# M from fp16 halves of Wo and of a kv divided by the K sums, M seven steps behind kv, and f2 of tile 62 in two halves

## The reference

```python
q = elu(q) + 1.0;  k = elu(k) + 1.0          # of layernorm(x) @ Wq, @ Wk
k_sum = k.sum(axis=2)                         # over the 2048 positions
z = einsum('bhnd,bhd->bhn', q, k_sum)[..., None] + EPS
kv = einsum('bhnd,bhne->bhde', k, v)
out = einsum('bhnd,bhde->bhne', q, kv) / z
x = x + out_heads_joined @ Wo + bo
h = square(relu(layernorm(x) @ W_fc.T));  y = h @ W_proj.T
for _ in range(5):                            # mem starts at 0
    mem_new = 0.9 * mem + y - reset;  spk = mem_new > 1
x = x + mean of the five spk
```

## Time and profile before

| | before |
|---|---|
| median of 3 runs | 1036.79 us (1036.23 to 1037.36) |
| the profiled execution | 1036.43 us, its span 1034.6 us |
| TensorE busy | 1026.2 us (99%) |
| VectorE busy | 873.8 us (84%) |
| ScalarE busy | 737.3 us (71%) |
| GpSimd busy | 654.7 us (63%) |

### The profile page before, as it was taken

How to read it: one execution, slowest core, us unless ns; L and a number is a source line. 1 busy time by engine, 2 the same in 40 slices (tenths; PEclk the granted TensorE clock), 3 DMA queues, 4 the chain that set the end, 5 groups by cost and what they waited for, 6 DMA issues and landing times.

```text
span 1034.6 us, 19797 instructions
## 1 busy us (share of the span) xinstructions
PE 1026.2 (99%) x6999; PEld 653.0 (63%) x6999; DVE 873.8 (84%) x1871; ACT 737.3 (71%) x1216; POOL 654.7 (63%) x410
## 2 busy tenths in 40 slices
PE   8999999999999999999999999999999999999998
PEld 4444444444444467777777767777777777777887
DVE  7899887898888699888888888888888888888875
ACT  8888677778768758676666767676767676676664
POOL 1444434455345488777778676878777777777835
PEclk9999999999999999999999999999999999999999
DMA  4546553225323545454454454455444444544441
GB/s 132 148 127 145 121 122 88 77 63 122 87 69 82 122 76 113 93 107 99 96 128 108 82 105 95 105 106 98 97 108 108 93 103 107 108 93 93 78 80 45
DMA packets 265284, 104.24 MB, mean 101 GB/s; under 512 B 219360, under 2 KB 262624, under 8 KB 265184
## 3 DMA queue, kind: packets, MB, share of 16 engines
q1 hardware_dynamic: 265040, 102.90, 44.7%
q10 hardware_dynamic: 144, 0.07, 0.0%
HBM read 33.69 MB, written 16.79 MB: 49 GB/s over the span
## 4 chain that ended last, share of the span: by engine, by line
PE 97%; DMA 1%; DVE 1%; ACT 1%; issue 0%; ACTq 0%; DVEq 0%
PE proj L619 31%; PE acc L784 16%; PE acc L820 16%; PE acc L662 15%; PE acc L759 8%; PE acc L768 4%; PE acc L761 4%; PE proj L696 1%; PE proj L684 1%; DMA xT<-xnat 1%; ACT feat L879 0%; PE acc L633 0%; PE proj L673 0%; DMA x_t<-in_L_attn_x_dram 0%; ACT feat L875 0%
## 5 line engine op out<-in xcount | busy, mean ns | idle before, releaser
L875 ACT ACTIVATE feat<-proj 128x1024 f32<-128x1024 f32 x123 | 125.7, 1022 | 193.7 <-PE proj L619 193.7
L1555 POOL TENSOR_TENSOR qT<-qT,feat 128x1024 f32<-128x1024 f32 x60 | 142.4, 2373 | 174.8 <-DVE xnat L1186 151.3
L1590 POOL TENSOR_TENSOR h<-h_f,h 128x512 f16<-128x512 f32 x128 | 148.8, 1183 | 159.2 <-ACT h L1052 159.2
L784 PE MATMUL acc<-xn2T,wfcT 128*128 128x256 f16 x1536 | 178.0, 273 | 0.0
L820 PE MATMUL acc<-wpT,h 128*128 128x256 f16 (+1 forms) x1560 | 177.9, 271 | 0.1
L662 PE MATMUL acc<-feat,xnat 128*128 128x512 f16 x768 | 176.2, 379 | 0.0
L619 PE MATMUL proj<-wk,xT 128*128 128x512 f16 x756 | 173.3, 379 | 0.7 <-DMA xT<-xnat 0.4
L784 PEld LDWEIGHTS acc<-xn2T,wfcT 128*128 128x128 f16 x1536 | 150.3, 98 | 28.9
L1561 POOL TENSOR_TENSOR feat<-feat,rz 128x1024 f32<-128x1024 f32 x60 | 165.8, 2764 | 2.8 <-DVE rz L1293 2.8
L619 PE MATMUL proj<-wq,xT 128*128 128x512 f16 x720 | 165.2, 379 | 0.0
L820 PEld LDWEIGHTS acc<-wpT,h 128*128 128x128 f16 x1560 | 150.6, 98 | 22.7 <-issue 0.3
(11 more groups left out here) (106 smaller groups left out, 1317.9 us busy)
## 6 DMA issues: line engine op xcount, KB each, us to landing
x_t<-in_L_attn_x_dram SPq DMA_DIRECT2D x128, 128.0 KB, 2.3
xT_spill<-xT SPq DMA_DIRECT2D x64, 128.0 KB, 2.0
out_dram<-out_t SPq DMA_DIRECT2D x63, 128.0 KB, 2.1
xT<-xT_spill SPq DMA_DIRECT2D x60, 128.0 KB, 2.3
ks_all<-ks_rows SPq DMA_DIRECT2D x4, 512.0 KB, 4.5
qT<-feat SPq DMA_TRANSPOSE x120, 3.1
m_all<-in_L_attn_Wk_dram SPq DMA_DIRECT2D x4, 256.0 KB, 4.3
xT<-xnat SPq DMA_TRANSPOSE x64, 2.4
```

Of the source, the lines that this page charges most:

```text
L784: mm = pe.matmul(acc[:, 2 + g % 2, f % 2 * 2 * P:(f % 2 + 1) * 2 * P], wfcT[:, left, f * C2 + c2, :], xn2T[:, pair % 4, right * C2 + c2, : ...
L1555: pool.tensor_tensor(kacc[:, b % 2, :], kacc[:, b % 2, :], k_feat(n), ALU.add).then_inc(k_added, 1)
L1590: pool.tensor_tensor(lo, h_f[:, k % 4, :], hi, ALU.subtract).then_inc(h_lo, 1)
```

## The change

Five things change.

1. `wo` is held as fp16 high and low part, split like the other weights in four pieces at steps 20 to 23 (one ScalarE and one VectorE instruction of 128x512 each), and its DMAs land in `stage`.
2. `kvT`, now with one buffer, is divided by the K sums before M. `load_ks` brings the K sums to all partitions one step behind their store. In step kv + 5 VectorE inverts 512 of them for each half of the partitions (`invert_ks`) and scales kv (`scale_kv`); in step kv + 6 ScalarE makes its high part and GpSimd the low part (`kv_hi_part`, `kv_lo_part`). In the second half the two inversions are at t = 16 and 17, the scaling at 18, the parts at 19. The transpose of the K sums, `rk` and `rks` go.
3. `m_job` makes 24 fp16 matmuls in place of 8 fp32 ones and waits for the low part of kv.
4. In `GUESTS` the M jobs stand seven and nine steps behind kv (before: two and four), the last batch's in `LATE` stay, and the q projections are at 24, 32, 40, 48 (before: 27, 33, 44, 49).
5. f2 of tile 62 is made like that of tile 63, in two halves of 128 columns in two banks (`f2_halves`, `f2_part`), its comparisons in the order of the last tile (`parted_spikes`).

```diff
-        GUESTS = {20: ("kv", 0, 0), 22: ("m", 0, 0), 24: ("m", 0, 1), 27: ("q", 0), 33: ("q", 1),
-                  36: ("kv", 1, 0), 38: ("m", 1, 0), 40: ("m", 1, 1), 44: ("q", 2), 49: ("q", 3),
-                  52: ("kv", 2, 0), 54: ("m", 2, 0), 56: ("m", 2, 1)}
+        GUESTS = {20: ("kv", 0, 0), 24: ("q", 0), 27: ("m", 0, 0), 29: ("m", 0, 1), 32: ("q", 1),
+                  36: ("kv", 1, 0), 40: ("q", 2), 43: ("m", 1, 0), 45: ("m", 1, 1), 48: ("q", 3),
+                  52: ("kv", 2, 0), 59: ("m", 2, 0), 61: ("m", 2, 1)}
...
             def m_job(b, i):
 
-                pe.wait_ge(chain_free, through("kv", b, 0))
+                pe.wait_ge(kv_lo, b + 1)
                 for qq in range(2):
-                    for s in range(2):
-                        for side in range(2):
-                            slot = 4 * s + 2 * i + qq
-                            own = slice(side * DH, (side + 1) * DH)
-                            mm = pe.matmul(m_half(b, i, side, qq)[s * DH:(s + 1) * DH, :],
-                                           kvT[own, b % 2, slot * DH:(slot + 1) * DH], wo[own, slot, :],
-                                           start=True, stop=True)
+                    for k, (left, right) in enumerate(PRODUCTS):
+                        for s in range(2):
+                            for side in range(2):
+                                slot = 4 * s + 2 * i + qq
+                                own = slice(side * DH, (side + 1) * DH)
+                                mm = pe.matmul(m_half(b, i, side, qq)[s * DH:(s + 1) * DH, :],
+                                               kv16[own, left, slot * DH:(slot + 1) * DH], wo[own, right, slot, :],
+                                               start=(k == 0), stop=(k == len(PRODUCTS) - 1), skip_group_check=True)
...
-                dve.transpose(kturn[:, :, :], ks_bank(b).rearrange("p (j r) -> p j r", r=32)
-                              ).then_inc(ks_turned, 1)
...
-                dve.wait_ge(ks_turned, b + 1)
-                dve.reciprocal(rk[:, b, :], kturn[:, :, 0]).then_inc(rk_ready, 1)
-                dve.wait_ge(rk_ready, b + 1)
-                dve.tensor_scalar(rks[:, b, :], rk[:, b, :], M_SCALE, None, ALU.mult).then_inc(rks_ready, 1)
...
+            def invert_ks(b, side):
+                own = slice(side * DH, (side + 1) * DH)
+                dve.wait_ge(ks_loaded[b], 16)
+                if b:
+                    dve.wait_ge(chain_full, through("m", b - 1, M_JOBS - 1))
+                dve.reciprocal(kv_share[own, :].rearrange("p (s j d) -> p s j d", s=2, d=DH),
+                               ks_at(b)[own, :].rearrange("p (j z s d) -> p z s j d", z=2, s=2, d=DH)[:, side]
+                               ).then_inc(kv_inverse, 1)
+
+            def scale_kv(b):
+                dve.wait_ge(kv_inverse, 2 * b + 2)
+                dve.wait_ge(chain_free, through("kv", b, 0))
+                dve.scalar_tensor_tensor(out=kvT[:, :], in0=kvT[:, :], scalar=KV_SCALE, in1=kv_share[:, :],
+                                         op0=ALU.mult, op1=ALU.mult).then_inc(kv_scaled, 1)
...
+                if kv_guest(n, 5) is not None:
+                    for side in range(2):
+                        invert_ks(kv_guest(n, 5), side)
+                    scale_kv(kv_guest(n, 5))
...
+                if t in (LAST_KV + 2, LAST_KV + 3):
+                    invert_ks(B - 1, t - LAST_KV - 2)
+                if t == LAST_KV + 4:
+                    scale_kv(B - 1)
...
+            def kv_lo_part(b):
+                pool.wait_ge(kv_hi, b + 1)
+                pool.tensor_tensor(kv16[:, LO, :], kvT[:, :], kv16[:, HI, :], ALU.subtract).then_inc(kv_lo, 1)
...
+                if n == PARTED:
+                    pe.wait_ge(h_lo, 4 * pair + 2)
+                    f2_part(n, 0, range(0, 6))
+                    f2_part(n, 1, range(0, 3))
+                    f2_part(n, 0, range(6, FB))
+                    f2_part(n, 1, range(3, FB))
```

More of the change, by code:

```diff
@@ L512, in _ @@
                     turn_weight(1, (n - 22) // 4, (n - 22) % 4, wpT)
[L513 to L516, removed]
+                if kv_guest(n, 2) is not None:
+                    store_ks(kv_guest(n, 2))
+                if kv_guest(n, 3) is not None:
+                    load_ks(kv_guest(n, 3))
                 if n == 34:
@@ L795, in f2_tile @@
                 pair, u = n // 2, n % 2
-                last = n == TILES - 2
                 if u == 0:
-                    pe.wait_ge(h_lo, 4 * pair + (2 if last else 4))
+                    pe.wait_ge(h_lo, 4 * pair + 4)
                 if n == 0:
@@ L806, in f2_tile @@
                     wait_past(pe, done, 5 * (before - HALVED))
-                if n == TILES - 1:
-                    pe.wait_ge(h_relu, 4 * pair + 4)
-                for half in range(2 if n == TILES - 1 else 1):
-                    i = 0
-                    for f in range(FB):
-                        if last and f >= FB // 2 and f % 2 == 0:
-                            pe.wait_ge(h_lo, 4 * pair + f // 2 + 1)
-                        for left, right in PRODUCTS:
-                            i += 1
-                            if n == TILES - 1:
-                                y, w = last_y(half), wpT[:, right, half * FB + f, :]
-                            else:
-                                y, w = y_at(n), wpT[:, right, f::FB, :]
-                            mm = pe.matmul(y, h[:, pair % 2, left, f, u * P:(u + 1) * P], w,
-                                           start=(i == 1), stop=(i == FB * len(PRODUCTS)))
-                    mm.then_inc(f2_done, 1)
+                i = 0
@@ new lines, in f2_tile, with f2_part @@
+                for f in range(FB):
+                    for left, right in PRODUCTS:
+                        i += 1
+                        mm = pe.matmul(y_at(n), h[:, pair % 2, left, f, u * P:(u + 1) * P], wpT[:, right, f::FB, :],
+                                       start=(i == 1), stop=(i == FB * len(PRODUCTS)))
+                mm.then_inc(f2_done, 1)
+            def f2_part(n, half, blocks):
+                pair, u = n // 2, n % 2
+                for f in blocks:
+                    if u == 0 and half == 0 and f >= FB // 2 and f % 2 == 0:
+                        pe.wait_ge(h_lo, 4 * pair + f // 2 + 1)
+                    for left, right in PRODUCTS:
+                        mm = pe.matmul(half_y(n, half), h[:, pair % 2, left, f, u * P:(u + 1) * P],
+                                       wpT[:, right, half * FB + f, :],
+                                       start=(f == 0 and (left, right) == PRODUCTS[0]),
+                                       stop=(f == FB - 1 and (left, right) == PRODUCTS[-1]))
+                if f == FB - 1:
+                    mm.then_inc(f2_done, 1)
@@ new lines, in f2_halves @@
+            def f2_halves(n):
+                pair = n // 2
+                pe.wait_ge(h_relu, 4 * pair + 4)
+                pe.wait_ge(spike_steps, 5 * HALVED)
+                for done in half_steps:
+                    pe.wait_ge(done, 5 * (n - 1 - HALVED))
+                if n == PARTED:
[4 more added lines that the diff above has]
+                    f2_part(n, 1, range(3, FB))
+                else:
+                    for half in range(2):
+                        f2_part(n, half, range(FB))
@@ L1008, in _ @@
                     m_hi_job(*which)
+                if kv_guest(n, 6) is not None:
+                    kv_hi_part(kv_guest(n, 6))
                 if n and live(n + 3):
```

82 lines of the change are left out of this document (52 added, 30 removed).

## The result

The changed kernel takes 1062.86 us (median of 6 runs, 1062.43 to 1064.93) against 1036.63 (6 runs, 1035.79 to 1037.36): a ratio of 1.0256, 95% interval 1.0243 to 1.0269. It is 26.2 us slower. The profiled execution took 1063.04, its span 1061.2; the span of before was 1034.6.

What follows compares the result with a forecast made beforehand. TensorE bounds the kernel, busy 1026.2 of 1034.6 us, so only stalls from other engines add. First-half stalls 21.2, second half 3.5, clock 4.0, M jobs -0.4 make 28.3: forecast 1065, range 1050 to 1072.

Steps and rivals of the forecast that it cites:

- 4.09 us: Time of one 64x512 VectorE reciprocal, extrapolated from the 16-element (242 ns) and 8-element (180 ns) rows at 7.75 ns an element.
- the chain's 6.35 (163.5 - 157.15): First and second batch: K projection held by VectorE's block, Newton, statistics and elu until 163.5, planned 157.15; stall 6.4 each.
- The 0.2 each: First and second batch: 0.2 us more for later steps, with q x K sums and M's low parts, making 6.6 each.
- the G product was to be 6.6 late: Third batch: the G product's operand 8.85 - 0.41 late against 1.8 of slack, a TensorE gap of 6.6 us.
- The further 1.4 us at the third batch: Third batch: low part of xn 8.44 late against 0.4 slack, so the next K projection starts 8.0 late in all.
- The second half: 3.5 predicted: Steps t = 16 to 18: two reciprocals make VectorE 5.2 late against 1.7 of slack, so f2 waits 3.5 us.
- The clock: 4.0 predicted: First half's three TensorE gaps bring back the 1.2 GHz level, 1.35 us a gap, 4.0 together.
- The rival by which it stays up: TensorE's clock does not fall behind the first half's gaps; without the 4.0: 1061, chance 0.22.
- The price of the start: Clock loss per gap taken from the kernel's start, 13 matmuls in 2.93 us read as 1.2 GHz: 1.35 us.
- -0.2 each: Second half: two M jobs of 24 fp16 matmuls, with no elu chain behind them, gain 0.2 us each.
- the edges of the M job go: Rival: fp32 causes the 0.46 us idle behind M jobs; eight jobs give 0.5 each, 1033, chance 0.03.
- Its new wait, for the low part of kv: M waits for GpSimd's low part of kv behind a sum of k; elu chain covers 0.2, counted 0.

Runs made afterwards that it cites:

- experiment 1: Changed kernel with each 64x512 reciprocal replaced by a copy of the same operands, so the division by the K sums is left out: 1039.28 us.
- experiment 4: Kernel before with only the first half's six 64x512 reciprocals added, seven steps behind kv, into a buffer nobody reads: 1059.62 us, ratio 1.0222.
- experiment 5: Changed kernel with the division put back to M (8 values per partition) and kv only scaled by a constant: 1037.85 us, ratio 1.0015.
- experiment 2: Changed kernel with zero-weight matmuls (64, 52, 52) filling TensorE's three gaps ahead of the waiting instruction: 1057.1 us, ratio 1.02.
- experiment 6: Changed kernel with division back at M, the elu behind each first-half M job halved, and K sums' store and load where they stood before: 1035.92 us.
- experiment 3: Changed kernel with the first half's second inversion and scaling one step later (kv + 6), parts and M jobs a step later too: 1057.89 us, ratio 1.0204.

## Why the prediction was right, and where its terms were off

**The mechanism held.** 1065 was predicted and 1062.86 measured. That the reciprocals cost, where, and through which instruction TensorE feels it, is shown by experiments 1, 4 and 5 from both sides: without the dear operation some 3 us are left, with it alone the loss is 23.

**The reciprocal was sized too dear.** 4.09 us were predicted, 3.35 measured. The two small rows, 180 and 242 ns, made 7.75 ns an element; from 16 to 512 elements it is (3347 - 242) / 496 = 6.3 ns. The difference of two short instructions had a 62 ns change stretched over 496 elements.
**A wait was missed that gave much of this back.** The reciprocals wait for the load of the K sums: 2.42, 0.68 and 0.64 us of idle time. The change moved the store and the load, and no term of my sum stands for the landing: the first load is issued at 138.87, behind the late transpose, and the first reciprocal starts at 142.66. Against the place where Newton would have started, one elu on, the reciprocals start 2.50, 0.77 and 0.72 late. At the first batch TensorE itself was 0.9 late by then, which leaves VectorE 0.34 more than in the earlier trace rows. So the chain's 6.35 (163.5 - 157.15) less 1.45, with 2.50 and less 0.34, is 7.06, and the gap is 7.0; at the second 6.35 - 1.45 + 0.77 is 5.7, as measured. The 0.2 each that I had added for later steps did not come. At the third the G product was to be 6.6 late, with 0.72 for 1.45 it is 5.9, as measured.

**The further 1.4 us at the third batch did not come.** The low part of xn was to hold the next K projection, 8.0 in all, as its slack was put at 0.4. That was read in the earlier trace rows from one step, and it was a special one: there the 512 KB load of the K sums goes out at 149.44, just ahead of the transpose at 150.53, whose projection starts 4.03 us later and has waited for it 0.39, where 2.4 is the median landing. In the step of the third batch before, the transpose went out at 353.07 and its projection started at 357.05: with 2.4 for the landing a slack of 1.6. In the changed kernel the low part ends at 356.30, which with 2.4 makes 358.7, and at full clock the projection was due at 356.02 + 2.59 = 358.61; at the lower clock it came at 360.51 and waited for nothing. In all the gaps came to 18.6 for 21.2.

**The second half: 3.5 predicted, 0.5 measured.** VectorE's residual was to be 5.2 late at the second reciprocal. f2 at 514.07 puts the next at 524.50 and the residual at 524.70; it came at 528.58, 3.9 late, as each reciprocal is 0.65 shorter. The rest is not the price but the assumption that lateness stays. q x K sums took 2.87 us at 506.80 and 1.22 at 531.49, 1.65 less, and the last spike operation was some 2.2 late against 1.7 of slack. In this kernel that line takes from 1.22 to 2.94 us. GpSimd beside it:

```profile
506.46 2.12 POOL L1632 TENSOR_TENSOR feat<-feat 128x1024 f16<-128x1024 f32 x1
...
518.21 1.91 POOL L1624 TENSOR_TENSOR feat<-feat,rz 128x1024 f32<-128x1024 f32 x1
...
519.60 1.61 DVE L1331 TENSOR_TENSOR feat<-feat,ks_all 128x1024 f32<-128x1024 f32 x1
...
531.49 1.81 POOL L1653 TENSOR_TENSOR x_t<-x_t,bo_all 128x256 f32<-128x256 f32 x1 [0.19 <-DMA x_t<-in_L_attn_x_dram]
```

The GpSimd instruction that runs when q x K sums starts ends 1.78 us later at 506.80 and 0.52 later at 519.60, and 1.78 + 1.09 is 2.87, 0.52 + 1.09 is 1.61. So it is in the whole second half: in 58 of the 60 rows of this line a GpSimd instruction is running at the start, and in 57 of them the row lasts for its rest and 1.07 to 1.13 us more (the 58th lies beside a merged row, from which the rest can't be read). In the two with none running it takes 1.22. At 531.49 both start together, and it is GpSimd's that is long, 1.81 us for a median of 0.74. In these rows the instruction that comes second stands until the first is through, and a late VectorE met another moment of GpSimd's list and got its lateness back. No run changed GpSimd's list to test this.

**The clock: 4.0 predicted, 6.1 in the trace, 5.8 by experiment 2.** The rival by which it stays up is out. The price of the start (13 matmuls, 1.35 us) was the wrong measure: behind the gaps the loss was 2.9, 1.3 and 1.9 us, the largest with about fourteen matmuls of 512 columns at half speed. Besides, that the start runs at the lower level was read from the spacing of its matmuls alone: the profile's granted clock is 1.00 there, from 2.92 to 5.80 us, in both kernels, so "the start agrees" has no clock row behind it. The Trainium skill (TensorE: Matmul & The Clock Gate; What's actually happening) has the throttled state as the default that activity lifts; the traces agree, with 0.50 granted behind 6.9 us of nothing and 1.00 where the same 7 us were filled.

**The M jobs.** In the second half -0.2 each was predicted and -0.24 measured. That the first half gets nothing from a shorter M, as the elu's chain covers it, is shown: 1.12 us in four of six with 24 fp16 matmuls as with 16 fp32 ones, 0.78 in all six once that elu is halved (experiment 6). The rival "the edges of the M job go" is refuted by the same rows. Its new wait, for the low part of kv, was counted at 0 and made the M job 0.8 late at the first batch: the sum of k ahead of it started only at 168.26, behind VectorE's low part of xn, and the low part of kv ended at 171.73, where M was due at 171.09. The elu for which another M job waits 1.06 us, at the second batch, is late since q x K sums stand in VectorE's list a step before it (1.21 us from 267.58), which is read from the timeline and was not tested; and the transpose that comes 0.9 late stands behind the four stores. These 2.8 us of the first half stood at nothing in my sum; -0.7 and -0.5 stand against them.

**The sum.** Predicted 21.2 + 3.5 + 4.0 - 0.4 = 28.3; measured 18.6 + 0.5 + 6.1 + 2.8 - 0.7 - 0.5 - 0.5 (M in the second half) + 0.3 ahead of the first batch - 0.1 at the end = 26.5 of 26.6. The stalls were 5.6 too dear, clock and small waits 4.9 too cheap. That the total lies nearer than its terms is luck; that the reciprocals on VectorE stop TensorE three times, and the clock falls behind it, is not.

## What to carry to other kernels

Divide where the divisor has fewest values: 8 per partition cost 180 ns, the same sums broadcast to 1024 cost 6.7 us in one place, and what a block on a side engine costs the main one is its length less the slack of what that engine must deliver next (at the third batch 2.2 us: 0.4 that VectorE was idle and 1.8 by which the low part of k was early). Shortening a job gains nothing while its follower waits on a chain through other engines (0.34 us per M job until the elu was halved), and each wait that is removed must be followed to the next: here from GpSimd's order to SyncE's. In an in-order queue count what stands ahead of the urgent item, four small stores being 2.75 us.

## What the runs showed that I had not expected

- A fp32 reciprocal runs at 6.3 ns an element per partition (3347 ns for 64x512), 8 times the copy of the same shape (424 ns).
- Matmuls with weights of zero are enough to keep the clock granted at 1.00 through a gap of 7 us.
- Behind a gap of 3.0 us the mean granted clock of the next twelve matmuls was 0.60 to 0.63, three times in one trace (experiment 3), and behind gaps of 5.0 to 7.0 us the loss was 1.3 to 2.9 us without following their length.
- q x K sums on VectorE lasts 1.1 us and the rest of whatever GpSimd instruction is running when it starts.
- 24 fp16 matmuls of 256 columns in 64x64 tiles take 0.78 us to the next job, 16 fp32 instructions of the same shape 1.02.
